# Sixteen-head attention: weighing as one two-operand instruction per head, output rounding on GpSimd, and a new order on VectorE

## The chip, the core and the metric

The kernel runs on one core of one Trainium2 chip. The metric is the device time of one execution in microseconds (us). Five engines work side by side, each through its own list of instructions in order: TensorE (PE in the profile; PEld is its weight load), VectorE (DVE), ScalarE (ACT), GpSimd (POOL) and SyncE (SP), which issues the transfers. They are ordered among each other by semaphores alone.

## What is computed

The reference is a chain of four conditioned blocks on `x` of 16 batches x 256 rows x 256 columns. The change touches the second block alone, its attention with 16 heads of 64 columns:

```python
q, k, v = jnp.split(x @ W_qkv, 3, axis=-1)              # 16 heads of 64
attn = jnp.einsum('bqhd,bkhd->bhqk', q, k) * 64 ** -0.5
attn = jax.nn.softmax(attn, axis=-1)
out = jnp.einsum('bhqk,bkhd->bqhd', attn, v).reshape(16, 256, 1024)
x = x + g_msa * (out @ W_out + b_out)
```

The other blocks (dense layers with gelu, a last attention with one head) are the same before and after.

## The kernel before

The whole program is unrolled in eight phases; the sixteen-head attention is phase 2 (`L1_ATTN`, `A` in the code). It runs over 16 batches, and in each over 8 pairs of heads: 128 periods, period `n = 8 * b + j` for batch `b` and pair `j`. Each engine has one function that writes out its work of one period (`mh_tensor`, `mh_scalar`, `mh_vector`, `mh_gpsimd`), and their statements are the order of each engine's queue. Matrix products keep float32 accuracy by splitting each operand in a rounded part (`hi`) and the rest (`lo`) and summing three products (`split3`), so each product's input has a rounding step and a subtracting step.

The software pipeline of a pair `n` runs through several periods:

- TensorE computes the scores of pair `n + 2` (`pair_scores`, L1028) between two turns of transposing the weighed probabilities of pair `n` (`pair_transpose`, L1105: turn 0 waits for `prob_ready` and for `pt_lo` of the pair before). Then come the projections of the next queries, keys and values (`proj_tensor`, L289 to L291): one item in periods j = 0, 3, 4 and 7, two items in j = 1, 2, 5 and 6 (`PROJ_AT`). Last come the output projection of pair `n - 3` (`out_pair`) and probabilities times values of pair `n - 1` (`values_pair`, L1131). The scores of a pair have one buffer, so `pair_scores` also waits for the exponentials of the pair before (`exp_ready`).
- ScalarE, in this order: `o_read(n - 2)` (L1148, two instructions that copy half of each head's output from PSUM to `oc`; it waits for `values_pair`), `pt_read` of the two heads (L1115), `score_exp` of the two heads of pair `n + 2` (L1055, four instructions, which also give the row sums; it waits for `score_max`), in j = 3 `rows_scalar` for the next batch (L1221) between the two heads, and `proj_scalar` of the period's items (L995, L1003).
- VectorE, in this order: `prob_inverse(n + 1)` (L1064, 1/sum), in j = 3 `res_vector` (L1186), `score_max(n + 2)` (L1045, the negated row maximum; it waits for the scores), `o_add(n - 2)` (L1157, two additions into `of`, which wait for both `o_corr` of `o_read`; then L1161, the rounding into `oT` hi), `pt_rest` of the two heads (L1120), in j = 3 `rows_vector` (L1232, L1235), `proj_vector` of the items (L1012, L1017), and layer norm or weight work in some periods (j = 1: `ln_stats`; j = 2: `ln_norm`; j = 4: `weights_hi`, L327).
- GpSimd, in this order: `prob_weigh` of the two heads of pair `n + 1` (L1083, in place, two instructions a head of 128 rows x 256 columns, each with one factor per row; it waits for `rinv_ready`), `o_rest(n - 2)` (L1166, the `lo` part of `oT`), and in some periods layer norm, residual and weight work (L366, L368, L1204, L1196, L334).

`rinv` and `nmax` have two buffers (`of_head` picks by pair), `prob` four (one per head), `of` and `oc` one. A period's order on an engine is fixed: an instruction that waits holds everything behind it on that engine.

Of the kernel before, what the change touches and what calls it, by code (L numbers as in the profile page):

```python
# [15 lines left out]
ALU = mybir.AluOpType  # L16
# [7 lines left out]
P = 128  # L24
BATCH, SEQ, D = 16, 256, 256
TPB = SEQ // P
# [17 lines left out]
def bass_cond_blocks(nc, t, out):  # L44
# [62 lines left out]
    with ctx:  # L107
        def sb(name, shape, dt=F32, scope=ctx):
            return scope.enter_context(nc.sbuf_tensor(name, shape, dt))

        def sem(name):
            return ctx.enter_context(nc.semaphore(name))
# [40 lines left out]
        prob = [sb(f"prob{i}", [P, TPB, SEQ], scope=att) for i in range(2)]  # L153
# [3 lines left out]
        of = sb("of", [P, SEQ], scope=att)  # L157
# [3 lines left out]
        oT = [[sb(f"oT{k}{i}", [P, SEQ], F32R, att) for k in ("hi", "lo")] for i in range(2)]  # L161
# [6 lines left out]
        rinv = [sb(f"rinv{i}", [P, 2 * TPB], scope=att) for i in range(2)]  # L168
# [65 lines left out]
        prob_ready = sem("prob_ready"); prob_ready1 = sem("prob_ready1"); pt_mm = sem("pt_mm"); pt_hi = sem("pt_hi")  # L234
        pt_lo = sem("pt_lo"); pv_mm = sem("pv_mm"); o_hi = sem("o_hi"); o_lo = sem("o_lo")
        out_mm = sem("out_mm"); ay_taken = sem("ay_taken"); axb_ready = sem("axb_ready")
# [102 lines left out]
        def sets(p, b):  # L339

            after_one = p == L1_ATTN + 1 and early(b, 1)
            return 1 if p == L1_ATTN or after_one else GB
# [27 lines left out]
        def ln_norm(eng, p, b, j):  # L370
            u = p * BATCH + b
            eng.wait_ge(ln_rstd, u + 1)
            if not early(u, sets(p, b)):
                eng.wait_ge(ln_tp, u + 1 - sets(p, b))
            for k in range(TPB):
                last = eng.tensor_scalar(xn[j][:, k * D:(k + 1) * D], x[:, bass.ds(b * ROWW + k * D, D)],  # L376
                                         meanvar[:, j, k, 0:1], rstd[:, j, k:k + 1], ALU.subtract, ALU.mult)
            last.then_inc(ln_xn, 1)
# [62 lines left out]
        def early(n, k):  # L441

            return isinstance(n, int) and n < k
# [505 lines left out]
        def item(own, what):  # L949

            i = [w for _, w in ITEMS].index(what)
            return NAHEAD + NPROJ * (own - 1 if ITEMS[i][0] >= NEXT else own) + i

        def items(b, j):

            own = b + 1 if j >= NEXT else b
            return [(own, what) for what in PROJ_AT[j]] if own < BATCH else []

        def v_heads(tile, half):

            cols = vv[:, tile, half * 4 * VP:(half + 1) * 4 * VP].rearrange("p (j w d) -> p j w d", w=4, d=DH)
            return cols[:, :, 0:4:3, :], cols[:, :, 1:3, :]
# [42 lines left out]
        def proj_vector(dve, own, what):  # L1005

            k = item(own, what)
            src = PROJ[k % 2]
            dve.wait_ge(proj_hi, k + 1)
            if what[0] == "qk":  # L1010
                hi, lo = qk[(PAIRS * own + what[1]) % 2]
                dve.tensor_tensor(lo[:, :], src[:, :], hi[:, :].bitcast(F32), ALU.subtract).then_inc(proj_lo, 1)  # L1012
            else:
                _, half, tile = what
                heads4 = src[:, :].rearrange("p (j h d) -> p j h d", h=2, d=DH)
                hi, lo = v_heads(tile, half)
                dve.tensor_tensor(lo, heads4, hi.bitcast(F32), ALU.subtract).then_inc(proj_lo, 1)  # L1017
# [18 lines left out]
        def of_head(tiles, h):  # L1036

            return tiles[h // 2 % 2][:, h % 2 * TPB:(h % 2 + 1) * TPB]
# [20 lines left out]
        def prob_inverse(dve, n):  # L1059

            dve.wait_ge(exp_ready, 2 * n + 2)
            if n >= 2:
                dve.wait_ge(prob_ready, 2 * n - 2)
            dve.reciprocal(rinv[n % 2][:, :], rsum[n % 2][:, :]).then_inc(rinv_ready, 2)  # L1064
# [14 lines left out]
        def prob_weigh(pool, h):  # L1079

            pool.wait_ge(rinv_ready, h - h % 2 + 2)
            for q in range(TPB):
                last = pool.tensor_scalar(prob[h % 4][:, q, :], prob[h % 4][:, q, :], of_head(rinv, h)[:, q:q + 1], None, ALU.mult)  # L1083
            last.then_inc(prob_ready, 1)

        def pair_transpose(pe, n, turn):

# [59 lines left out]
                main, rest, cols = o_halves(j)  # L1147
                act.activation(oc[main, :], OB[rest, cols], ACT.Copy).then_inc(o_corr, 1)  # L1148

        def o_add(dve, pair, i):  # L1150

            if pair:
                dve.wait_ge(o_lo, pair)
            for j in range(2):
                main, _, cols = o_halves(j)
                dve.wait_ge(o_corr, 2 * pair + 2)
                dve.tensor_tensor(of[main, :], OB[main, cols], oc[main, :], ALU.add).then_inc(o_sum, 1)  # L1157
            dve.wait_ge(o_sum, 2 * pair + 2)
            if pair >= 2:
                dve.wait_ge(out_mm, pair - 1)  # L1160
            dve.tensor_copy(oT[i][0][:, :], of[:, :]).then_inc(o_hi, 1)  # L1161

        def o_rest(pool, pair, i):

            pool.wait_ge(o_hi, pair + 1)
            pool.tensor_tensor(oT[i][1][:, :], of[:, :], oT[i][0][:, :].bitcast(F32),  # L1166
                               ALU.subtract).then_inc(o_lo, 1)
# [11 lines left out]
        def res_vector(dve, p, b, src, done, count, n):  # L1179

            dve.wait_ge(done, count)
            dve.wait_ge(agate_loaded[n % 2], 16 * (n // 2 + 1))
            if n:
                dve.wait_ge(ax_new, n)
            row = agate[n % 2][:, 0:D].unsqueeze(1).to_broadcast([P, TPB, D])
            dve.tensor_tensor(aupd[:, :].rearrange("p (k d) -> p k d", k=TPB),  # L1186
                              src[:, :].rearrange("p (k d) -> p k d", k=TPB), row, ALU.mult
                              ).then_inc(ay_taken, 1)
# [49 lines left out]
        PERIODS = PAIRS * BATCH  # L1238
# [65 lines left out]
        def mh_vector(dve, b, j):  # L1304

            n = PAIRS * b + j
            if n + 1 < PERIODS:
                prob_inverse(dve, n + 1)
            if j == 3 and b:
                res_vector(dve, A, b - 1, YB, out_mm, PAIRS * b, b - 1)  # L1310
            if n + 2 < PERIODS:
                score_max(dve, n + 2)
            if n >= 2:
                o_add(dve, n - 2, n % 2)
            for h in range(2):
                pt_rest(dve, 2 * n + h)
            if j == NEXT - 1 and b + 1 < BATCH:
                rows_vector(dve, b + 1)
            for it in items(b, j):
                proj_vector(dve, *it)  # L1320
            if b + 1 < BATCH:
                if j == 1:
                    ln_stats(dve, A, b + 1, 0)
                if j == 2:
                    ln_norm(dve, A, b + 1, 0)
            if j == NEXT:
                weights_hi(dve, A + 1, b)
            if b == BATCH - 1 and j == NEXT - 1:
                head_norms("vector", dve, A + 1)
            if b == BATCH - 1 and j == PAIRS - 2:  # L1330
                dve.wait_ge(pt_mm, HEADS * BATCH - 2)
                for k in range(GB):
                    head_unit("vector", dve, A + 1, k)
            if n == PERIODS - 1:
                o_add(dve, n - 1, (n - 1) % 2)
                o_add(dve, n, n % 2)
                res_vector(dve, A, b, YB, out_mm, PAIRS * b + PAIRS, b)

        def mh_gpsimd(pool, b, j):
# [31 lines left out]
        def mh_start(name, eng):  # L1371
            if name == "gpsimd":
                for h in range(2):
                    prob_weigh(eng, h)
                return
            f = {"tensor": proj_tensor, "scalar": proj_scalar, "vector": proj_vector}[name]

            def head_pair(n):
                if name == "vector":
                    score_max(eng, n)  # L1380
                if name == "scalar":
                    for h in (2 * n, 2 * n + 1):
                        score_exp(eng, h)

            f(eng, 0, ("qk", 0))
            f(eng, 0, ("qk", 1))
            if name == "tensor":
                pair_scores(eng, 0)
            head_pair(0)
            f(eng, 0, ("v", 0, 0))  # L1390
            f(eng, 0, ("qk", 2))
            if name == "tensor":
                pair_scores(eng, 1)
            if name == "vector":
                prob_inverse(eng, 0)
            head_pair(1)
            f(eng, 0, ("v", 0, 1))
            f(eng, 0, ("qk", 3))

        def mh_phase(eng, body):  # L1400

            for b in range(BATCH):
                for j in range(PAIRS):
                    body(eng, b, j)
# [398 lines left out]
```

## Time and profile before

| | us |
|---|---|
| median of 3 runs | 1752.8 (1749.63 to 1753.22) |
| span of the profiled execution | 1752.5 |
| sixteen-head attention within it | about 256 to 1016 |
| PE busy / PEld busy, whole span | 1626.4 (93%) / 1458.4 (83%) |
| DVE busy | 1294.3 (74%) |
| ACT busy | 1179.8 (67%) |
| POOL busy | 1093.6 (62%) |

The profile is one execution. Busy shares are averages over all phases; the stage of the change has to be read by itself. A PE that is called busy is not PE at its peak, because ends of matmuls are modelled and overlap: the starts of successive matmuls are what counts. In a timeline, "x2" means two instructions in a row that were merged in one line, and the bracket gives the idle time ahead of an instruction and what ended it.

### The profile page before, as it was taken

What the parts mean: (1) busy time and instruction counts of PE and PEld (TensorE: products, weight loads), DVE (VectorE), ACT (ScalarE), POOL (GpSimd) and SP (SyncE); (2) the same over time, 40 slices, a digit from 0 to 9 for tenths busy, and PEclk for the clock granted to TensorE, in tenths of its full rate; (3) what the DMA queues carried; (4) which work ended last, traced back from release to release, by engine and by line L of the source; (5) the groups of instructions that cost most, each with busy time, mean ns of one, the idle gap of its engine ahead of it and who ended that gap; (6) DMA issues with size and microseconds to landing.
All of it is one profiled execution on the core that took longest, in us unless ns stands there. A gap on an engine that the chain in (4) does not pass through costs nothing.

```text
span 1752.5 us, 37390 instructions
## 1 busy us (share of the span) xinstructions
PE 1626.4 (93%) x13251; PEld 1458.4 (83%) x13251; DVE 1294.3 (74%) x2766; ACT 1179.8 (67%) x2896; POOL 1093.6 (62%) x1261
## 2 busy tenths in 40 slices
PE   4888998999999999999999789999999999989997
PEld 2557878888888888888888779999888889989997
DVE  3767768989898888888888745556788778864442
ACT  2545657777787777787777655556676667666663
POOL 1555667888888888888888622333555568842223
PEclk7999999999999999999999899999999999999999
DMA  8213310000000000000000011111122112221111
GB/s 306 61 49 86 88 42 11 11 10 11 11 7 6 11 10 11 11 11 11 10 11 10 1 32 30 31 31 32 48 57 58 45 27 46 47 52 37 37 49 48
DMA packets 110973, 65.93 MB, mean 38 GB/s; under 512 B 81530, under 2 KB 92788, under 8 KB 110788
## 3 DMA queue, kind: packets, MB, share of 16 engines
q1 hardware_dynamic: 110788, 63.54, 13.3%
q8 instruction: 107, 1.75, 0.4%
q14 instruction: 78, 0.64, 0.1%
HBM read 59.06 MB, written 4.46 MB: 36 GB/s over the span
## 4 chain that ended last, share of the span: by engine, by line
PE 64%; DVE 13%; issue 8%; POOL 6%; ACT 2%; DMA 0%; DVEq 0%; POOLq 0%; SPq 0%; ACTq 0%
PE bank L289 14%; PE bank L290 13%; PE bank L291 13%; POOL prob L1083 5%; PE s_banks L289 4%; PE bank L1105 4%; DVE ptlo L1120 4%; PE s_banks L290 4%; PE s_banks L291 4%; PE s_banks L1028 4%; PE bank L1131 3%; DVE of L1157 2%; PE bank L417 2%; DVE xn L376 2%; DVE oThi L1161 1%
## 5 line engine op out<-in xcount | busy, mean ns | idle before, releaser
L1083 POOL TENSOR_SCALAR prob<-prob,rinv 128x256 f32<-128x256 f32 x508 | 465.8, 935 | 117.0 <-DVE rinv L1064 117.0
L1055 ACT ACTIVATE prob<-s_banks,nmax 128x256 f32<-128x256 f32 x512 | 236.6, 475 | 17.4 <-DVE nmax L1045 17.4
L289 PE MATMUL bank<-WBhi,hl 128*128 128x256 f32 x768 | 219.0, 285 | 6.2 <-DVE upd L647 5.3
L290 PE MATMUL bank<-WBlo,hh 128*128 128x256 f32 x768 | 217.7, 283 | 0.0
L291 PE MATMUL bank<-WBhi,hh 128*128 128x256 f32 x768 | 215.5, 281 | 0.0
L1115 ACT ACTIVATE pthi<-bank 128x512 fp32r<-128x512 f32 x256 | 139.2, 596 | 100.9 <-PE bank L1105 98.8
L1045 DVE TENSOR_REDUCE nmax<-s_banks 128x4 f32<-128x1024 f32 x128 | 156.0, 1219 | 62.6 <-issue 61.9
L610 ACT ACTIVATE hh<-bank,vecs 128x512 fp32r<-128x512 f32 x120 | 82.9, 691 | 155.7 <-PE bank L291 155.7
L430 ACT ACTIVATE nThi<-bank,mod 128x256 fp32r<-128x256 f32 x192 | 110.5, 575 | 104.9 <-issue 75.7
L289 PE MATMUL bank<-aThi,WAlo 128*128 128x256 f32 x576 | 175.4, 304 | 0.6 <-DVE aTlo L438 0.2
L1120 DVE TENSOR_TENSOR ptlo<-bank,pthi 128x512 fp32r<-128x512 f32 x256 | 164.9, 686 | 4.0
L616 DVE TENSOR_TENSOR hl<-bank,hh 128x512 fp32r<-128x512 f32 x120 | 82.5, 688 | 112.3 <-ACT bank L610 111.2
L290 PE MATMUL bank<-aTlo,WAhi 128*128 128x256 f32 x576 | 161.6, 281 | 0.0
L289 PEld LDWEIGHTS bank<-WBhi,hl 128*128 128x128 f32 x768 | 145.8, 190 | 18.7 <-issue 9.7
L291 PE MATMUL bank<-aThi,WAhi 128*128 128x256 f32 x576 | 161.1, 280 | 0.0
L1105 PE MATMUL bank<-ident,prob 64*128 64x64 f32 x2048 | 113.9, 228 | 45.2 <-DVE ptlo L1120 23.4
L290 PEld LDWEIGHTS bank<-WBlo,hh 128*128 128x128 f32 x768 | 145.8, 190 | 7.2
L1105 PEld LDWEIGHTS bank<-ident,prob 64*128 64x128 f32 x2048 | 92.6, 139 | 67.1 <-POOL prob L1083 37.1
L376 DVE TENSOR_SCALAR xn<-x,meanvar,rstd 128x256 f32<-128x256 f32 x224 | 123.6, 610 | 31.4 <-POOL rstd L368 31.4
L291 PEld LDWEIGHTS bank<-WBhi,hh 128*128 128x128 f32 x768 | 146.5, 191 | 0.0
L1131 PE MATMUL bank<-ptlo,vv 128*128 128x256 f32 x512 | 129.8, 286 | 7.2 <-DVE of L1157 7.2
L616 DVE TENSOR_TENSOR hl<-s_banks,hh 128x512 fp32r<-128x512 f32 x120 | 81.6, 680 | 72.6 <-ACT s_banks L610 72.6
(185 smaller groups left out, 5546.5 us busy)
## 6 DMA issues: line engine op xcount, KB each, us to landing
gates<-gate_scratch SPq DMA_DIRECT2D x96, 256.0 KB, 3.6
agate<-gate_scratch SPq DMA_DIRECT2D x32, 256.0 KB, 3.6
stage<-in_L_cond_W SPq DMA_DIRECT2D x64, 64.0 KB, 2.3
out<-x SPq DMA_DIRECT2D x16, 256.0 KB, 2.2
adaw<-in_L_cond_Wc SPq DMA_DIRECT2D x1, 3072.0 KB, 17.7
stage<-in_L_cond_W_qkv SPq DMA_DIRECT2D x8, 384.0 KB, 3.4
x<-in_x SPq DMA_DIRECT2D x1, 2560.0 KB, 16.6
stage<-in_L_cond_ff_w SPq DMA_DIRECT2D x32, 64.0 KB, 2.2
```

Source lines behind the costliest of these rows:

```text
L289: pe.matmul(dst, lhs[1], rhs[0], start=start, stop=False, skip_group_check=True)
L290: pe.matmul(dst, lhs[0], rhs[1], start=False, stop=False, skip_group_check=True)
L291: return pe.matmul(dst, lhs[0], rhs[0], start=False, stop=stop, skip_group_check=True)
L376: last = eng.tensor_scalar(xn[j][:, k * D:(k + 1) * D], x[:, bass.ds(b * ROWW + k * D, D)], meanvar[:, j, k, 0:1], rstd[:, j, k:k + 1], AL ...
L616: dve.tensor_tensor(hl[r][:, :], U_BANKS[r][:, :], hh[r][:, :].bitcast(F32), ALU.subtract).then_inc(h_lo, 1)
L1045: dve.tensor_reduce(nmax[n % 2][:, :], s_banks[:, :, :].rearrange("p h (q k) -> p (h q) k", q=TPB), AX_X, ALU.max, negate=True).then_inc(n ...
L1055: last = act.activation(prob[h % 4][:, q, :], SB_[h % 2][:, q * SEQ:(q + 1) * SEQ], ACT.Exp, bias=of_head(nmax, h)[:, q:q + 1], accum_out= ...
L1083: last = pool.tensor_scalar(prob[h % 4][:, q, :], prob[h % 4][:, q, :], of_head(rinv, h)[:, q:q + 1], None, ALU.mult)
L1105: both.append(pe.transpose(PTB[h][:, at:at + HALF], prob[(2 * n + h) % 4][rows, q, c * P:(c + 1) * P], ident[rows, rows]))
L1115: act.activation(pt[h % 4][0][:, :], PTB[h % 2][:, :], ACT.Copy).then_inc(pt_hi, 1)
L1120: dve.tensor_tensor(pt[h % 4][1][:, :], PTB[h % 2][:, :], pt[h % 4][0][:, :].bitcast(F32), ALU.subtract).then_inc(pt_lo, 1)
L1131: last = pe.matmul(OB[:, h % 2 * SEQ:(h % 2 + 1) * SEQ], vv[:, c, h * P:(h + 1) * P], pt[h % 4][m][:, c * SEQ:(c + 1) * SEQ], start=c == 0 ...
```

## The change

Three edits, all in phase 2:

- `prob_weigh` issues one two-operand multiplication per head over 128 x 512 (the probabilities times `rinv`, whose one value per row and tile is repeated along 256 columns) in the place of two multiplications of 128 x 256 by a factor per row.
- The rounding of `of` into `oT` hi moves from the end of `o_add` on VectorE to the start of `o_rest` on GpSimd, with its waits (`o_sum`, `out_mm`).
- VectorE's order: `o_add(n - 2)` stands ahead of `score_max(n + 2)`; `prob_inverse` is done for pair `n + 2` in place of `n + 1`, after `pt_rest` and the layer norm work and ahead of `proj_vector`, which now stands behind `ln_stats` and `ln_norm`. The inverse of pair 1 is done at the end of the stage's start.

```diff
         def prob_weigh(pool, h):
             pool.wait_ge(rinv_ready, h - h % 2 + 2)
-            for q in range(TPB):
-                last = pool.tensor_scalar(prob[h % 4][:, q, :], prob[h % 4][:, q, :], of_head(rinv, h)[:, q:q + 1], None, ALU.mult)
-            last.then_inc(prob_ready, 1)
+            scale = of_head(rinv, h).unsqueeze(2).to_broadcast([P, TPB, SEQ])
+            pool.tensor_tensor(prob[h % 4][:, :, :], prob[h % 4][:, :, :], scale, ALU.mult).then_inc(prob_ready, 1)
...
-        def o_add(dve, pair, i):
+        def o_add(dve, pair):
...
                 dve.tensor_tensor(of[main, :], OB[main, cols], oc[main, :], ALU.add).then_inc(o_sum, 1)
-            dve.wait_ge(o_sum, 2 * pair + 2)
+
+        def o_rest(pool, pair, i):
+
+            pool.wait_ge(o_sum, 2 * pair + 2)
             if pair >= 2:
-                dve.wait_ge(out_mm, pair - 1)
-            dve.tensor_copy(oT[i][0][:, :], of[:, :]).then_inc(o_hi, 1)
-
-        def o_rest(pool, pair, i):
-
+                pool.wait_ge(out_mm, pair - 1)
+            pool.tensor_copy(oT[i][0][:, :], of[:, :]).then_inc(o_hi, 1)
             pool.wait_ge(o_hi, pair + 1)
...
         def mh_vector(dve, b, j):
             n = PAIRS * b + j
-            if n + 1 < PERIODS:
-                prob_inverse(dve, n + 1)
             if j == 3 and b:
                 res_vector(dve, A, b - 1, YB, out_mm, PAIRS * b, b - 1)
+            if n >= 2:
+                o_add(dve, n - 2)
             if n + 2 < PERIODS:
                 score_max(dve, n + 2)
-            if n >= 2:
-                o_add(dve, n - 2, n % 2)
             for h in range(2):
                 pt_rest(dve, 2 * n + h)
             if j == NEXT - 1 and b + 1 < BATCH:
                 rows_vector(dve, b + 1)
-            for it in items(b, j):
-                proj_vector(dve, *it)
             if b + 1 < BATCH:
                 if j == 1:
                     ln_stats(dve, A, b + 1, 0)
                 if j == 2:
                     ln_norm(dve, A, b + 1, 0)
+            if n + 2 < PERIODS:
+                prob_inverse(dve, n + 2)
+            for it in items(b, j):
+                proj_vector(dve, *it)
             if j == NEXT:
                 weights_hi(dve, A + 1, b)
...
             f(eng, 0, ("qk", 3))
+            if name == "vector":
+                prob_inverse(eng, 1)
```

## Rows read from the trace of the kernel before

**Rows 1.** The stage, by stretches: us; busy PE, PEld, DVE, ACT, POOL; clock, DMA, GB/s.

```profile
256.00:1000.00 744.00, 693.42 (x7233) 642.08 (x7231) 656.14 (x1262) 583.56 (x1744) 620.33 (x727) 0.99 0.05 10
```

**Rows 2.** Waits in that stretch: who for whom, us in total, times, longest.

```profile
POOL prob L1083 <- DVE rinv L1064: 117.0, 95, 6.2
DVE nmax L1045 <- issue: 61.9, 82, 2.0
```

**Rows 3.** One line that runs once per batch, with first and last start.

```profile
L1235 DVE TENSOR_TENSOR aTlo<-bank,aThi x15: 691/691/692, 282.8 to 934.6; 128x512 fp32r<-128x512 f32 x15
```

**Rows 4.** Timeline of PE, batch 8, j = 5 to 7: turn 0's start.

```profile
660.81 0.46 PE L1105 MATMUL bank<-ident,prob 64*128 64x64 f32 x8 [0.67 <-POOL prob L1083]
...
666.87 0.46 PE L1105 MATMUL bank<-ident,prob 64*128 64x64 f32 x8
...
672.93 0.46 PE L1105 MATMUL bank<-ident,prob 64*128 64x64 f32 x8
...
678.21 0.46 PE L1105 MATMUL bank<-ident,prob 64*128 64x64 f32 x8 [0.55 <-DVE ptlo L1120]
```

**Rows 5.** Timeline of ACT, batch 8, j = 3 to 5: start, length, instruction.

```profile
652.97 1.02 ACT L1221 ACTIVATE aThi<-bank,mod 128x256 fp32r<-128x256 f32 x2
653.87 0.48 ACT L1055 ACTIVATE prob<-s_banks,nmax 128x256 f32<-128x256 f32 x1
...
658.07 0.47 ACT L1055 ACTIVATE prob<-s_banks,nmax 128x256 f32<-128x256 f32 x1 [0.65 <-DVE nmax L1045]
...
659.89 0.61 ACT L995 ACTIVATE qkhi<-bank 128x512 fp32r<-128x512 f32 x1
660.52 0.79 ACT L1148 ACTIVATE oc<-bank 64x256 f32<-64x256 f32 x2
...
665.24 0.61 ACT L995 ACTIVATE qkhi<-bank 128x512 fp32r<-128x512 f32 x1
665.72 0.62 ACT L1003 ACTIVATE vv<-bank 128x512 fp32r<-128x512 f32 x1
```

**Rows 6.** Timeline of DVE, batch 8, j = 3 to 5.

```profile
650.24 0.65 DVE L1186 TENSOR_TENSOR aupd<-bank,agate 128x512 f32<-128x512 f32 x1
650.82 1.21 DVE L1045 TENSOR_REDUCE nmax<-s_banks 128x4 f32<-128x1024 f32 x1
...
656.84 1.20 DVE L1045 TENSOR_REDUCE nmax<-s_banks 128x4 f32<-128x1024 f32 x1
...
660.52 0.69 DVE L1012 TENSOR_TENSOR qklo<-bank,qkhi 128x512 fp32r<-128x512 f32 x1
661.13 0.55 DVE L327 CAST WBhi<-stage 128x128 fp32r<-128x128 f32 x2
...
662.17 1.23 DVE L1045 TENSOR_REDUCE nmax<-s_banks 128x4 f32<-128x1024 f32 x1 [0.40 <-issue]
```

**Rows 7.** Timeline of the stage's end, the last pair, on ACT, DVE and POOL.

```profile
1012.48 0.78 ACT L1148 ACTIVATE oc<-bank 64x256 f32<-64x256 f32 x2 [2.35 <-PE bank L1131]
...
1013.36 0.87 DVE L1157 TENSOR_TENSOR of<-bank,oc 64x256 f32<-64x256 f32 x2 [1.92 <-ACT oc L1148]
...
1014.64 0.72 POOL L1166 TENSOR_TENSOR oTlo<-of,oThi 128x256 fp32r<-128x256 f32 x1 [2.40 <-DVE oThi L1161]
```

**Rows 8.** Groups of instructions by shape: busy us, mean ns of one, idle before.

```profile
L1083 POOL TENSOR_SCALAR prob<-prob,rinv 128x256 f32<-128x256 f32 x508 | 465.8, 935 | 117.0 <-DVE rinv L1064 117.0
L1166 POOL TENSOR_TENSOR oTlo<-of,oThi 128x256 fp32r<-128x256 f32 x128 | 94.1, 735 | 13.5 <-DVE oThi L1161 13.5
L334 POOL TENSOR_TENSOR WBlo<-stage,WBhi 128x128 fp32r<-128x128 f32 x96 | 42.8, 468 | 35.3 <-DVE WBhi L327 35.3
L1204 POOL TENSOR_TENSOR x<-aupd,axb 128x512 f32<-128x512 f32 x32 | 41.2, 1288 | 2.3 <-DVE aupd L1186 2.3
L1777 POOL MEMSET ident<- 128x128 f32 x1 | 0.2, 204 | 0.0
L1161 DVE CAST oThi<-of 128x256 fp32r<-128x256 f32 x128 | 47.2, 369 | 4.4
```

More of the change, by code:

```diff
@@ L1334, in mh_vector @@
             if n == PERIODS - 1:
-                o_add(dve, n - 1, (n - 1) % 2)
-                o_add(dve, n, n % 2)
+                o_add(dve, n - 1)
+                o_add(dve, n)
                 res_vector(dve, A, b, YB, out_mm, PAIRS * b + PAIRS, b)
```

## The prediction

> **What bounds the kernel now.** I read the stage by itself first. From 256 to 1000 us PE is busy 693 of 744 us, DVE 656, POOL 620, ACT 584, at granted clock 0.99 [rows 1]: no single engine is far ahead, so order and waits decide. One line that runs once a batch starts 14 batches apart at 282.8 and 934.6 us [rows 3]: 651.8 / 14 = **46.56 us a batch**, 5.82 a period. Then the waits: GpSimd stands 117 us for 1/sum, and VectorE's maximum 62 us for scores ("issue" hides that name) [rows 2].
>
> Then PE's timeline for its floor [rows 4]. From 660.81 to 666.87 and on to 672.93 a period with two projection items takes 6.06 us with no idle time: there PE is the bound. The next, with one item, takes 5.28, of which 0.55 is idle; less the 0.07 by which modelled ends overlap the next start where nothing waits, 5.28 - 0.55 - 0.07 = 4.66. Four of each make 42.9 us a batch, and the transposes of the next batch's rows some 0.5 (an estimate: as one turn's 0.46 [rows 4]): 43.4. So about 3.1 us a batch are stalls that waits cause: for weighed probabilities (0.67) or for `pt_lo` (0.55) [rows 4], both in light periods (one item).
>
> The question is which loop of waits replaces these. I followed ACT's and DVE's queues in time [rows 5, 6].
>
> **The change part by part.**
>
> *Weighing.* Two instructions of 0.935 = 1.87 us a head go, one over 128 x 512 with two operands comes [rows 8]. No row repeats one element along the columns; the nearest is a two-operand 128 x 512 at 1.29 (L1204). I take 1.29; the ends are 1.27 and 1.87 (as slow as the two now), and I see no row that excludes more. Here a rule speaks against the change. The trace has a one-input instruction at 0.935 / 256 = 3.7 ns a column and a two-input one at 1.29 / 512 = 2.5 [rows 8]. The Trainium skill (GPSIMD Engine Reference, 4.1 Engine selection) has it the other way round: one input near line rate, two inputs about half as fast. By it the merging would lose time on GpSimd; the rows disagree, and I go by them.
>
> *Rounding on GpSimd.* VectorE loses 0.37 us a pair. GpSimd gains a copy of 128 x 256 that no row shows: between 0.20 (a fill of half the columns) and 0.735 (the two-operand subtraction of that size); I take 0.47, near the middle, which is also what L334 takes for half the columns [rows 8]. With the 0.10 handover before and inside `o_rest`, GpSimd's sum for a batch is 16 x 1.29 + 8 x (0.47 + 0.735 + 0.3) + about 4.6 for the rest (two residual steps at 1.29, weights 2 x 0.47, layer norm about 1.1) = 37.3 us. It fits in 46.56, so both edits are **off the path**, until a weighing costs more than some 1.29 + 10 / 16 = 1.9 us. What is behind the new wait for `o_sum` on GpSimd is the next pair's weighing, which nobody needs until a period later.
>
> *1/sum two pairs ahead.* Sums of pair n + 2 exist when ACT ends its exponentials in period n. GpSimd then weighs a whole period before turn 0 needs it: the 117 us of waiting stop mattering, and so does the 0.67. The inverse stands ahead of `proj_vector`, which waits for ACT's item behind the same exponentials anyway: nothing is lost there.
>
> *Output sums first.* This is where I see the price. `o_add` waits for `o_read`, which ACT issues only behind the exponentials and items of the period before; the trace shows it at 660.52, straight behind the item [rows 5]. Today the maximum is ahead of `o_add` and needs just the scores. After the change maximum, exponentials, and all else on ACT stand behind `o_add`. That closes a loop, all of whose links have rows:
>
> - four exponentials, 658.07 to 659.89: 1.82 [rows 5]
> - the item, 659.89 to 660.52: 0.63; a second one adds 665.24 to 665.72, 0.48 [rows 5]
> - `o_read`: 0.79 [rows 5]
> - handover ACT to DVE, 1012.48 + 0.78 to 1013.36: 0.10 [rows 7]
> - `o_add`: 0.87 [rows 7]
> - maximum: 1.20 to 1.23, 1.21 [rows 6]
> - handover, 656.84 + 1.20 to 658.07: 0.03 [rows 5, 6]
>
> Sum 5.45 us in light periods, 5.93 in heavy ones (PE's 6.06 there is not a bound of its own, as PE has gained time in the light periods). Four of each: 45.5. On top, once a batch: `rows_scalar` between the exponentials, 652.97 to 653.87, 0.90 [rows 5]; `res_vector` (0.65) and `weights_hi` (0.55) [rows 6] now stand ahead of an `o_add`. VectorE ends the item's rest 0.61 + 0.03 + 0.69 = 1.33 after the item's start, and `oc` is there at 0.63 + 0.79 + 0.10 = 1.52, so 0.19 of each is covered: 0.46 and 0.36. `rows_vector` pushes one item by some 0.1 (estimate). That is 1.82, and **47.3 us a batch** against 46.56.
>
> *The end.* The last pairs' copy lies on the path: 0.47 in place of 0.37 plus a handover of 0.10, for three pairs 0.6 us [rows 7, 8].
>
> Sum: 0.78 x 15.5 batches (128 periods less the first and last few) = 12 us, + 0.6. The profiled span 1752.5 is 0.3 under the median of 1752.8, so both serve: **1765 us**.
>
> What could change a link: VectorE may overlap `o_add` and maximum a little, ACT may start `o_read` a little sooner; 0.1 a period either way is 0.8 a batch, 12 us.
>
> **The rivals.**
>
> 1. *PE becomes the bound (faster).* In heavy periods the maximum waits for scores today (0.40 us at 662.17 [rows 6]; 62 us in all [rows 2]), and `oc` of 660.52 is there at 661.31, 0.86 us ahead of it: `o_add` would fill a hole and cost nothing. If `o_read` comes before the scores in light periods too, all 3.1 us of stalls a batch go: 1752.5 - 48 = 1704. It decides where the loop is under 5 us; half of that gain gives 1728. Against it: the links sum to 5.45, none has 0.4 us to give, and ACT's order isn't touched. The room itself can be judged otherwise: PEld is busy 642 of 744 us [rows 1]. The Trainium skill (Perfetto Trace Analysis, Identifying the Most-Contended Engine) trusts this share over matmul busy time; by it the room would be 102 us and the time near 1650, where the start-to-start rows leave 48.
> 2. *Nothing to measure.* Every link at its lowest takes 0.1 off a period: 46.5 a batch, 1752.
> 3. *Weighing is dear.* If repeating one element costs twice 1.29, GpSimd needs 37.3 + 20.6 = 57.9 us a batch and is the bound: + 176, 1930. It decides from 1.9 us a head. No row speaks for it but the missing one.
> 4. *The inverse isn't early*: were it held behind VectorE's work, weighing would still have a period's slack, and the loop is the same.
>
> **How the numbers follow.** Forecast (loop) 0.59; rival 1 with its partial forms 0.20; rival 2 0.16; rival 3 0.05. Two runs of this kernel can tell about 0.2% (3.5 us) from no change: faster 0.20, same 0.16, slower 0.64. Range: the loop 12 us either way is 1753 to 1777; for contention of GpSimd's copy with VectorE and for a dearer copy I add 8 above, and below I go to 1742, where rival 1's weak form lies.
>
> **What would show it.** Right: in the waits of the stage DVE L1157 waits for ACT L1148 in almost all periods, DVE's maximum waits for nothing else, ACT L1055 waits for L1045 by some 1 us a period; PE idles at L1028 for exponentials in place of L1105 for L1083; the once-a-batch line comes every 47.3 us. POOL: 1.29 a head, no wait of PE on it. Wrong: L1157 doesn't wait, or light periods are at 4.7 to 5.2 us (rival 1); POOL has no idle time and L1105 waits for it (rival 3).

## The result, and the profile after

The changed kernel takes 1763.28 us (median; 1761.94 to 1765.67) against 1751.89 for the kernel before in the same session: ratio **1.0072, 95% interval 1.006 to 1.0084**: 0.7% slower, clear of the scatter. 1765 was forecast. The profiled execution after spans 1760.1 us.

The stage by itself, 256 to 1000 us, columns as in [rows 1]:

```profile
256.00:1000.00 744.00, 691.02 (x7149) 639.51 (x7148) 620.42 (x1125) 576.71 (x1714) 454.51 (x588) 1.00 0.05 10
```

GpSimd's busy time fell from 620 to 455 us, VectorE's from 656 to 620, and in the same 744 us PE got through fewer matmuls (7149 for 7233). All engines have more idle time than in [rows 1]: the mark of a longer loop of waits, not of a fuller engine. The line that runs once a batch, as in [rows 3]:

```profile
L1234 DVE TENSOR_TENSOR aTlo<-bank,aThi x15: 691/691/693, 280.5 to 944.0; 128x512 fp32r<-128x512 f32 x15
```

663.5 / 14 = **47.39 us a batch** in place of 46.56 (forecast 47.3). The waits of the stage (who for whom, us, times, longest), which answer to [rows 2]:

```profile
POOL prob L1083 <- DVE rinv L1064: 213.0, 95, 6.2
ACT prob L1055 <- DVE nmax L1045: 131.4, 124, 2.1
...
PE s_banks L1028 <- ACT prob L1055: 25.3, 62, 1.1
...
PEld bank L1104 <- POOL prob L1083: 8.6, 2, 7.1
...
DVE of L1156 <- ACT oc L1147: 6.4, 32, 0.4
```

ScalarE now waits for the maximum in nearly every period (131.4 / 124 = 1.06 us); PE waits for exponentials ahead of its scores; weighed probabilities hold it twice in all. GpSimd still waits for 1/sum, and longer, but a period ahead of need. The loop itself, on ScalarE's timeline (batch 8, periods j = 3 to 6; compare [rows 5]; the first two lines belong to j = 3):

```profile
653.61 0.78 ACT L1147 ACTIVATE oc<-bank 64x256 f32<-64x256 f32 x2
...
659.80 0.62 ACT L995 ACTIVATE qkhi<-bank 128x512 fp32r<-128x512 f32 x1
...
663.52 0.48 ACT L1055 ACTIVATE prob<-s_banks,nmax 128x256 f32<-128x256 f32 x1 [1.06 <-DVE nmax L1045]
...
665.33 0.61 ACT L995 ACTIVATE qkhi<-bank 128x512 fp32r<-128x512 f32 x1
665.97 0.78 ACT L1147 ACTIVATE oc<-bank 64x256 f32<-64x256 f32 x2
666.89 1.09 ACT L1114 ACTIVATE pthi<-bank 128x512 fp32r<-128x512 f32 x2
669.02 0.48 ACT L1055 ACTIVATE prob<-s_banks,nmax 128x256 f32<-128x256 f32 x1 [1.04 <-DVE nmax L1045]
...
670.83 0.61 ACT L995 ACTIVATE qkhi<-bank 128x512 fp32r<-128x512 f32 x1
671.31 0.62 ACT L1003 ACTIVATE vv<-bank 128x512 fp32r<-128x512 f32 x1
...
676.82 0.61 ACT L995 ACTIVATE qkhi<-bank 128x512 fp32r<-128x512 f32 x1
```

and on VectorE's (compare [rows 6]; the first two lines belong to j = 3):

```profile
654.33 0.68 DVE L1185 TENSOR_TENSOR aupd<-bank,agate 128x512 f32<-128x512 f32 x1
654.93 0.86 DVE L1156 TENSOR_TENSOR of<-bank,oc 64x256 f32<-64x256 f32 x2
...
665.98 0.69 DVE L1012 TENSOR_TENSOR qklo<-bank,qkhi 128x512 fp32r<-128x512 f32 x1 [0.26 <-ACT qkhi L995]
666.58 0.35 DVE L327 CAST WBhi<-stage 128x128 fp32r<-128x128 f32 x2
666.85 0.88 DVE L1156 TENSOR_TENSOR of<-bank,oc 64x256 f32<-64x256 f32 x2
667.76 1.23 DVE L1045 TENSOR_REDUCE nmax<-s_banks 128x4 f32<-128x1024 f32 x1
```

Read round once: exponentials 663.52 to 665.33, item to 665.97, `o_read` to 666.75, sums at 666.85, maximum 667.76 to 668.99, next exponentials 669.02. Item to item is 665.33 to 670.83 = **5.50 us** with one item, 670.83 to 676.82 = **5.99** with two. What GpSimd got, by shape (busy us, mean ns, idle before; compare [rows 8]):

```profile
L1083 POOL TENSOR_TENSOR prob<-prob,rinv 128x512 f32<-128x512 f32 x254 | 260.1, 1042 | 213.5 <-DVE rinv L1064 213.5
...
L1165 POOL TENSOR_TENSOR oTlo<-of,oThi 128x256 fp32r<-128x256 f32 x128 | 94.7, 740 | 10.3
...
L1163 POOL CAST oThi<-of 128x256 fp32r<-128x256 f32 x128 | 51.1, 399 | 31.2 <-DVE of L1156 31.2
```

### The profile page after: what moved, and what is told of

Its sections match the earlier page's. It is cut to its first block and busy times, and to the rows that moved or that the text cites. A ratio compares the mean times of both kernels' runs of the same rounds, so it can differ in the third digit from the quotient of the medians.

```text
span 1760.1 us, 37136 instructions
## 1 busy us (share of the span) xinstructions
PE 1629.0 (93%) x13251; PEld 1460.1 (83%) x13251; DVE 1263.3 (72%) x2638; ACT 1182.8 (67%) x2896; POOL 937.5 (53%) x1135
## 5 line engine op out<-in xcount | busy, mean ns | idle before, releaser
L1083 POOL TENSOR_TENSOR prob<-prob,rinv 128x512 f32<-128x512 f32 x254 | 260.1, 1042 | 213.5 <-DVE rinv L1064 213.5
L610 ACT ACTIVATE hh<-s_banks,vecs 128x512 fp32r<-128x512 f32 x120 | 84.3, 703 | 72.5 <-PE s_banks L291 71.7
```

Source lines behind the costliest of these rows:

```text
L610: last = act.activation(dst[:, :], U_BANKS[r][:, :], ACTF[p], bias=vecs[:, at:at + 1])
L1083: pool.tensor_tensor(prob[h % 4][:, :, :], prob[h % 4][:, :, :], scale, ALU.mult).then_inc(prob_ready, 1)
```

## The experiments

My theory: the sums ahead of the maximum close the loop above, and it alone is the price. Rivals: the copy and its waits on GpSimd cost it; the inverse's new place does (VectorE idles 58.7 us ahead of it); or VectorE's amount of work decides. "us a batch" is always from the first and the last start of the once-a-batch line; ratios are to the kernel before in the same session.

| run | median us | ratio (95% interval) | us a batch |
|---|---|---|---|
| changed kernel | 1763.3 | 1.0072 (1.006 to 1.0084) | 47.39 |
| e1 changed, maximum first | 1717.3 | 0.9823 (0.9808 to 0.9838) | 44.31 |
| e2 before, sums first alone | 1788.4 | 1.0227 (1.0212 to 1.0243) | 48.95 |
| e3 before, weighing alone | 1747.1 | 0.9994 (0.9981 to 1.0006) | 46.44 |
| e4 before, inverse alone | 1745.2 | 0.9973 (0.9959 to 0.9987) | 46.24 |
| e5 changed, rounding on VectorE in the loop | 1823.0 | 1.0412 (1.0394 to 1.043) | 51.14 |
| e6 changed, rounding on VectorE behind it | 1761.5 | 1.0063 (1.0048 to 1.0079) | 47.26 |
| e7 before, rounding on GpSimd alone | 1728.8 | 0.9878 (0.9863 to 0.9893) | 45.26 |
| e8 e1, rounding on VectorE | 1733.5 | 0.9901 (0.9883 to 0.9919) | 45.55 |
| e9 e1, `rows_scalar` later | 1726.0 | 0.9868 (0.9853 to 0.9883) | 45.12 |
| e10 before, rounding and weighing | 1716.6 | 0.9813 (0.9798 to 0.9828) | 44.41 |
| e11 before, rounding and inverse, maximum first | 1716.4 | 0.9812 (0.9793 to 0.9832) | 44.35 |

**e1: one thing undone.**

```diff
-            if n >= 2:
-                o_add(dve, n - 2)
             if n + 2 < PERIODS:
                 score_max(dve, n + 2)
+            if n >= 2:
+                o_add(dve, n - 2)
```

> The changed kernel with one thing undone: score_max stands ahead of o_add again. Loop theory: the maximum needs the scores alone, o_add is off the loop, PE is the bound with 4.7 to 4.9 us in a light period and 6.06 in a heavy one, 43.4 to 44.2 us a batch: 1704 to 1717 us, well below both kernels. Rival (the copy on GpSimd, its two waits, or the inverse ahead of the items is what costs): 1758 or more, about as the changed kernel.

Measured 1717.34 us, 0.3 above the theory's range (44.31 us a batch against 43.4 to 44.2) and 46 us below the changed kernel, for swapping two statements. Turn 0's starts on PE (timeline of batch 8: the beginnings of j = 6, of j = 7 and of the next batch's j = 0; compare [rows 4]):

```profile
647.74 0.46 PE L1104 MATMUL bank<-ident,prob 64*128 64x64 f32 x8
...
653.80 0.47 PE L1104 MATMUL bank<-ident,prob 64*128 64x64 f32 x8
...
658.62 0.46 PE L1104 MATMUL bank<-ident,prob 64*128 64x64 f32 x8
```

6.06 us with two items, 4.82 with one, and no idle time in a bracket: PE's own rhythm, 44.31 us a batch against the floor of 43.4 worked out ahead. Between 300 and 900 us PE waits neither for weighed probabilities nor for `pt_lo`. In the same 600 us PEld is busy 554, 92%. The weight-load share that the Trainium skill prefers to matmul busy time (Perfetto Trace Analysis, Identifying the Most-Contended Engine) would still leave 8% here; the matmul starts leave some 2%, and no run found more.

**e2: the same statement's order alone, on the kernel before.**

```diff
+            if n >= 2:
+                o_add(dve, n - 2)
             if n + 2 < PERIODS:
                 score_max(dve, n + 2)
             if n >= 2:
-                o_add(dve, n - 2, n % 2)
+                o_round(dve, n - 2, n % 2)
```

> The kernel before with one part of the change alone: the two additions of o_add ahead of the maximum; the rounding stays on VectorE, behind the maximum. Loop theory: the same loop of 5.5 and 6.0 us, and as the layer norm work still stands behind the items, some 1.9 us more a batch in j = 1 and 2: about 49 us a batch, 1785 to 1800. Rival (the order costs nothing by itself, the rest of the change does): 1745 to 1755.

Measured 1788.37, 48.95 us a batch, as the theory had it. The order alone costs 39 us on the kernel before, where no copy on GpSimd and no moved inverse exist. So the rivals that put the price there fall; the rest of the change in fact pays 25 us of it back.

**e3 and e4: weighing alone, inverse alone.**

```diff
-            for q in range(TPB):
-                last = pool.tensor_scalar(prob[h % 4][:, q, :], ...)
+            pool.tensor_tensor(prob[h % 4][:, :, :], prob[h % 4][:, :, :], scale, ALU.mult).then_inc(prob_ready, 1)
```

> The kernel before with the two-operand weighing alone. Loop theory: 0.83 us less a head on GpSimd (1.04 in place of 1.87) ends the waits of PE for weighed probabilities, VectorE's queue stays the bound of light periods: 45.7 to 46.3 us a batch, 1737 to 1749. Rival (the two-operand form disturbs VectorE): 1753 or more.

```diff
-            if n + 1 < PERIODS:
-                prob_inverse(dve, n + 1)
...
+            if n + 2 < PERIODS:
+                prob_inverse(dve, n + 2)
             for it in items(b, j):
                 proj_vector(dve, *it)
```

> The kernel before with the inverse two pairs ahead and the new place of proj_vector alone. Loop theory: GpSimd weighs a period ahead, PE waits for pt_lo alone: 45.5 to 46.3 us a batch, 1735 to 1748. Rival (the inverse holds proj_vector, as the 59 us of idle time before it in the changed kernel suggest): 1757 or more.

1747.06, the same as before within its interval, and 1745.20, 0.27% faster. Both times lie in the theory's ranges, at their slow ends; e3's 46.44 us a batch lies above its 45.7 to 46.3. Of PE's waits for weighed probabilities (between 300 and 900 us of the kernel before PEld waits 24.3 us, 41 times) e3 leaves none and e4 10.3 us, 13 times, once a batch. The wait for `pt_lo` of [rows 4] stands right behind them. These are the waits of e3's stage between 300 and 900 us:

```profile
DVE nmax L1045 <- issue: 46.4, 65, 1.0
...
PE bank L1104 <- DVE ptlo L1119: 23.3, 52, 0.5
```

The rival of e3 is right once a batch. In j = 2 the rounding's cast on VectorE falls beside a two-operand weighing (batch 9, VectorE's line and GpSimd's):

```profile
690.32 1.15 DVE L1160 CAST oThi<-of 128x256 fp32r<-128x256 f32 x1
```

```profile
690.28 1.04 POOL L1083 TENSOR_TENSOR prob<-prob,rinv 128x512 f32<-128x512 f32 x1
```

In the kernel before, the cast of that period takes 0.29. From the start of one maximum to the start of the next, in the mean of 12 batches, j = 2 takes 6.93 us in e3 and 6.54 before, and VectorE's timeline shows no idle time in it (688.28 to 695.22). These 0.39 us take back most of the 0.55 that the four light periods gain together.

**e5 and e6: one instruction in the loop and out of it.** Both are the changed kernel with the rounding back on VectorE:

```diff
             if n >= 2:
                 o_add(dve, n - 2)
+                o_round(dve, n - 2, n % 2)      # e5: here
             if n + 2 < PERIODS:
                 score_max(dve, n + 2)
+            if n >= 2:
+                o_round(dve, n - 2, n % 2)      # e6: here in its place
```

> The changed kernel with the rounding back on VectorE, between the two additions and the maximum, so inside the loop. Loop theory: 0.33 to 0.42 us more in every period, none of it covered: 2.6 to 3.4 us a batch, 1803 to 1816. Rival (VectorE's amount of work decides, not its place): the same time as e6.

> The same instruction on the same engine, but behind the maximum, so outside the loop. Loop theory: VectorE has idle time there (0.73 us before the inverse), so nothing: 1760 to 1771. Rival (amount of work): 40 us or more above the changed kernel, as e5.

e6: 1761.52, no more than the changed kernel. e5: 1822.97, 60 us more. The same work on the same engine costs nothing behind the maximum and 3.75 us a batch ahead of it, so VectorE's amount of work does not decide; its place in the loop does. e5 came out 7 us above its range. VectorE's timeline in e5 (batch 8, j = 0 and then j = 4), with GpSimd's line beside the latter:

```profile
667.53 0.88 DVE L1156 TENSOR_TENSOR of<-bank,oc 64x256 f32<-64x256 f32 x2 [0.18 <-ACT oc L1147]
668.44 0.29 DVE L1163 CAST oThi<-of 128x256 fp32r<-128x256 f32 x1
668.77 1.23 DVE L1045 TENSOR_REDUCE nmax<-s_banks 128x4 f32<-128x1024 f32 x1
...
694.52 0.88 DVE L1163 CAST oThi<-of 128x256 fp32r<-128x256 f32 x1
695.42 1.22 DVE L1045 TENSOR_REDUCE nmax<-s_banks 128x4 f32<-128x1024 f32 x1
```

```profile
693.20 2.04 POOL L1083 TENSOR_TENSOR prob<-prob,rinv 128x512 f32<-128x512 f32 x2 [3.09 <-DVE rinv L1064]
```

The cast takes 0.29 us alone and 0.88 beside the weighing, which ended at 695.24, 0.16 ahead of the cast's end. The group's mean in this kernel:

```profile
L1163 DVE CAST oThi<-of 128x256 fp32r<-128x256 f32 x114 | 49.6, 435 | 3.9
```

8 x (0.435 + 0.03 between two instructions) = 3.7 us a batch, against 3.75 measured. I had priced it at 0.33 to 0.42; what I left out is the cast beside a weighing.

**e7: rounding on GpSimd alone.**

```diff
-            dve.tensor_copy(oT[i][0][:, :], of[:, :]).then_inc(o_hi, 1)
+            pool.tensor_copy(oT[i][0][:, :], of[:, :]).then_inc(o_hi, 1)     # in o_rest, with its waits
```

> The kernel before with the rounding on GpSimd alone. Loop theory: VectorE's light periods lose 0.4 us, but GpSimd then has two weighings of 1.87, a copy, a subtraction and handovers, 5.1 us a period and 4.6 a batch, and takes over as the bound: 45.8 to 46.6 us a batch, 1738 to 1751. Rival (GpSimd isn't a bound at that load): 44.9 a batch, 1725.

1728.81: below the range I gave, near the rival's 1725. GpSimd's timeline shows why:

```profile
657.77 3.64 POOL L1083 TENSOR_SCALAR prob<-prob,rinv 128x256 f32<-128x256 f32 x4
661.35 0.40 POOL L1164 CAST oThi<-of 128x256 fp32r<-128x256 f32 x1
661.84 0.74 POOL L1166 TENSOR_TENSOR oTlo<-of,oThi 128x256 fp32r<-128x256 f32 x1
662.56 3.63 POOL L1083 TENSOR_SCALAR prob<-prob,rinv 128x256 f32<-128x256 f32 x4
```

A period's work is 662.56 - 657.77 = 4.79 us, not the 5.1 I had with three handovers of 0.10: between copy and subtraction there is 0.09 and elsewhere none. What gains is VectorE's row from scores to `pt_rest`, which ends a light period and from which the cast is gone: PE's wait for `pt_lo`, 19.7 us in 39 times between 300 and 900 us of the kernel before, is not there in e7. GpSimd does hold PE at times (37.2 us, 77 times from 256 to 1000 us, "PEld bank L1105 <- POOL prob L1083"). That is what e1 gains beyond e7: e10 below differs from e7 in the weighing alone, gains the same 12 us, and has no such wait between 300 and 900 us.

**e8, e10, e11: which part makes e1's gain.** e8 is e1 with `o_round` behind `o_add` on VectorE; e10 is e7 with the weighing's edit of e3; e11 is e1 with the old weighing.

```diff
             if n >= 2:
                 o_add(dve, n - 2)
+                o_round(dve, n - 2, n % 2)      # e8, behind score_max
```

> e1 (changed kernel with the maximum first) with the rounding back on VectorE behind the additions. It asks how much of e1's gain is due to the rounding's move. Loop theory: in light periods VectorE's row from scores to pt_rest is the bound (4.80 us in e1), so 0.4 us more in each of four to five: 1.6 to 2 us a batch, 1740 to 1750. Rival (the move brings nothing, the weighing and the inverse did it): 1715 to 1720.

> The kernel before with the rounding on GpSimd and the two-operand weighing; the order of VectorE as before. It asks whether e1's gain needs the early inverse. Theory: with GpSimd at 3.3 us a period its wait for the inverse no longer holds turn 0: 44.3 to 44.8 us a batch, 1715 to 1725. Rival (the early inverse is needed): near e7, 45.3, 1728 or more.

> e1 with the old weighing of two instructions a head. It asks whether e1's gain needs the two-operand form. Theory: with the inverse ahead GpSimd (8 x 4.9 + 4.6 = 43.8 us a batch) evens out light and heavy periods and stays just under PE: 44.3 to 45.0, 1715 to 1727. Rival (at that load GpSimd is the bound): 45.3 or more, 1728 to 1740.

e8: 1733.45, between theory and rival, 16 us above e1: of e1's 32 us half hangs on the rounding's move. It cost 1.24 us a batch, not 1.6 to 2: from maximum to maximum, in the mean of 12 batches, the light periods j = 0, 3, 4 and 7 grew by 0.34, 0.24, 0.33 and 0.33, the heavy ones by 0.05 at most. e10 and e11: 1716.59 and 1716.39, both as e1. So the move of the rounding plus either of the other two parts gives the whole gain, and the third part brings nothing on top. These three are the fastest kernels here, 1.8% ahead of before.

**e9: a last 0.5 us a batch.** In e1 the scores of j = 4 start late, behind exponentials that `rows_scalar` had split.

```diff
-            if j == NEXT - 1 and b + 1 < BATCH:
-                rows_scalar(act, b + 1)
             if n + 2 < PERIODS:
                 score_exp(act, 2 * n + 5)
+            if j == NEXT - 1 and b + 1 < BATCH:
+                rows_scalar(act, b + 1)
```

> e1 with rows_scalar behind both heads' exponentials in place of between them. In e1 the scores of j = 4 start 0.54 us after turn 0 in place of 0.24, because exponentials end 0.9 us later in j = 3. Loop theory: 0.3 to 0.6 us a batch less than e1's 44.31: 1708 to 1714. Rival (rows_vector, now later, holds the projections of j = 4): the same as e1 or up to 0.9 us a batch more, 1717 to 1732.

The rival was right: 1726.00, 0.81 us a batch more than e1. PE's timeline in j = 4:

```profile
641.91 0.39 PE L289 MATMUL bank<-aThi,WAlo 128*128 128x256 f32 x1 [0.69 <-DVE aTlo L1234]
```

The next batch's projections wait for `rows_vector`, which came later with `rows_scalar`.

## Why the prediction held, step by step

- **The bound.** PE was not the limit of light periods and `pt_lo` stood behind the probabilities: e3 and e4 show both. The floor of 43.4 us a batch was reached within 0.9 (e1). In heavy periods the changed kernel takes 5.99 us, less than PE's 6.06 of [rows 4], so that was no bound of its own, as forecast.
- **The loop.** Forecast 5.45 and 5.93 us, measured 5.50 and 5.99. Link by link, in light periods: exponentials 1.81 (1.82 forecast), item 0.64 (0.63), `o_read` 0.78 (0.79), handover 0.10 (0.10), sums 0.91 (0.87), maximum 1.23 (1.21), handover 0.03 (0.03). The sums were mis-sized by 0.04: the maximum starts 0.03 behind their end.
- **Once a batch.** `res_vector`: `oc` was there at 654.39, 0.10 later the sums could have begun, they began at 654.93: 0.44 (0.46 forecast). `weights_hi` was priced at 0.36 and cost nothing: its two casts took 0.35 in place of 0.55, and j = 3 to j = 5 give 5.53 and 5.50 us from item to item. In the kernel before, GpSimd's subtraction for `oT` lo (660.73 to 661.46) ran beside the first cast, which took 0.41; in the changed kernel nothing of GpSimd ran beside them, and each took 0.22. `rows_vector` was priced at 0.1 and cost 0.03 (5.53 for 5.50). By luck these errors and that of the links (8 x 0.05) cancel: 4 x 5.50 + 4 x 5.99 + 0.90 + 0.44 = 47.3, measured 47.39.
- **The end and the total.** At the stage's end it takes 1.41 us from the last sums to the subtraction for `oT` lo (1023.22 to 1024.63) where it took 1.28 (1013.36 to 1014.64 [rows 7]): 0.13 a pair, 0.4 for three, where 0.6 was forecast. With 0.83 x 15.5 = 12.9 this makes 13.3 us, and the medians differ by 11.4. The 2 us between them are not explained; they lie within the spread of the changed kernel's runs (1761.94 to 1765.67). So that 1765 came within 0.1% of 1763.28 is in part luck, and the 47.3 us a batch is the better test.
- **GpSimd.** The weighing was taken at 1.29 us a head within 1.27 to 1.87; it took 1.04, outside those bounds. The copy was taken at 0.47 and took 0.40. Both are off the path: e6 shows it for the copy, and for the weighing e11 against e1 does, though with the maximum first. The Trainium skill (GPSIMD Engine Reference, 4.1 Engine selection) has GpSimd near line rate with one input and about half as fast as VectorE with two, by which the merging would have lost time. The trace does not agree: one instruction of two inputs over 512 columns, the second one repeated, takes 1.04 us, and the two one-input instructions took 2 x 0.935 [rows 8].
- **Signs.** ScalarE's wait for the maximum came as forecast. "DVE waits for ACT's `oc` in almost all periods" did not: 32 times, 6.4 us. The loop still goes through it, as VectorE's own item ends nearly together with it (665.98 + 0.69 = 666.67, the sums possible at 666.85), so little idle time is left to show. PE's wait for exponentials, 25 us, is there, and between 300 and 900 us PE waits for no weighed probabilities; its waits for `pt_lo`, 20.7 us from 256 to 1000, stay beside it, which the sign left out.
- **The rivals.** PE as the bound is what e1 gives, 1717 for the 1704 I worked out; it needs the maximum first. Dear weighing did not happen.

Not tried: a second buffer for `oc` and its bank, which would let `o_read` leave the loop with the sums still first.

## What to carry to other kernels

Before an instruction is moved ahead of another on one engine, list what it waits for on the other engine's queue: here the sums needed a copy that stands behind the exponentials, and the exponentials needed the maximum behind the sums, so the move closed a loop of 5.5 us where PE needs 4.8. Add the loop's links from start to start and compare with the busiest engine's period; that told the 47.39 us a batch to 0.1, while busy shares (all of them lower after) told nothing. Once one wait of several has been taken away, look for the one right behind it: the weighing and the inverse were worth 0 and 0.3% alone, and either of them the last third of 1.8% together with the rounding. And price an instruction by what will run beside it: the same cast took 0.29 us or 1.15.

## What the runs showed of the hardware

- A two-operand multiplication on GpSimd whose second operand repeats one element along 256 columns takes 1.04 us over 128 x 512; an addition with both operands dense takes 1.29 [rows 8].
- VectorE's cast from SBUF to SBUF (128 x 256) takes 0.29 us alone and up to 1.15 beside GpSimd's two-operand weighing: it ends 0.15 to 0.16 us behind the weighing (e3 in j = 2, above; e5 in j = 4; e6 in j = 5). Beside the one-input weighings of the kernel before it took 0.63 at most. The case of e6 from VectorE's timeline, where GpSimd's weighings end at 669.62:

```profile
668.73 1.04 DVE L1163 CAST oThi<-of 128x256 fp32r<-128x256 f32 x1
```

The Trainium skill (GPSIMD Engine Reference, 8. Key points) says that GpSimd shares its SBUF interfaces with VectorE, with contention for VectorE instructions in a 2-port mode or with two inputs from SBUF. The trace agrees that there is contention and gives the size, up to almost four times the cast's time; whether the cast, which has one input, runs in such a mode no run here shows.
